# An adaLN transformer block on one core: first transfers reordered, modulation products moved, next tile's input prepared one slot ahead

## The reference

```python
x = L0_attn_x                                             # (8, 1024, 512)
mod = (_silu(L0_c) @ L0_wmod).reshape(8, 6, 1, -1)        # one row per batch: 6 x 512
sa, ca, ga, sb, cb, gb = (mod[:, i] for i in range(6))
ga, gb = sign(g) * maximum(abs(g), 0.25)                  # for both gates
h = _layernorm(x) * (1 + ca) + sa
x = x + ga * attention(h)                                 # 16 heads of 32
h = _layernorm(x) * (1 + cb) + sb
x = x + gb * feed(h)                                      # dense + shared LoRA + 2 of 6 routed LoRAs
```

## Time and profile before

| | us |
|---|---|
| median of 3 runs | 2372.66 (2369.42 to 2372.81) |
| the profiled execution | 2375.0 |
| its span, first to last instruction | 2373.1 |
| PE busy | 2145.7 (90%) |
| DVE busy | 1749.7 (74%) |
| ACT busy | 1340.7 (56%) |
| POOL busy | 788.2 (33%) |

### The profile page before, as it was taken

One profiled execution on the slowest core, in us unless ns is written; L12 is line 12 of the kernel. 1 busy time (PEld: TensorE's weight loads), 2 busy tenths in 40 slices (PEclk: granted clock), 3 DMA queues, 4 the chain that ended last, 5 costly groups with the idle time before them and its releaser, 6 DMA issues.

```text
span 2373.1 us, 48974 instructions
## 1 busy us (share of the span) xinstructions
PE 2145.7 (90%) x17944; PEld 1427.3 (60%) x17944; DVE 1749.7 (74%) x4740; ACT 1340.7 (56%) x4701; POOL 788.2 (33%) x780
## 2 busy tenths in 40 slices
PE   4888999899998999989999899989999899997887
PEld 0665666566665666656665566656666566664454
DVE  3456888768886788768887688866887678875776
ACT  1244666556665566646656566655666556663664
POOL 0333333343333233333332433324333423333221
PEclk9998999999999999989999899999999999997989
DMA  6010000200011000110001100020001100011000
GB/s 233 19 40 15 23 28 24 68 22 28 28 32 63 28 24 28 46 49 19 28 28 41 54 28 24 23 76 24 22 25 45 50 28 28 24 46 45 19 19 19
DMA packets 48892, 89.64 MB, mean 38 GB/s; under 512 B 6760, under 2 KB 6760, under 8 KB 48656
## 3 DMA queue, kind: packets, MB, share of 16 engines
q1 hardware_dynamic: 39440, 69.74, 9.6%
q10 hardware_dynamic: 9216, 16.78, 1.9%
HBM read 69.68 MB, written 16.83 MB: 36 GB/s over the span
## 4 chain that ended last, share of the span: by engine, by line
PE 63%; DVE 22%; ACT 6%; issue 5%; POOL 2%; DMA 1%; SPq 0%; DVEq 0%; ACTq 0%; POOLq 0%
PE ps_m L702 9%; PE ps_o L634 7%; PE ps_m L506 6%; PE ps_m L667 5%; PE ps_m L507 5%; PE ps_m L508 5%; PE ps_s L628 4%; PE ps_t L610 4%; DVE ps_s L1548 4%; ACT pw L1033 3%; PE ps_m L684 3%; DVE wmax L1553 3%; PE ps_s L597 3%; PE ps_s L586 3%; PE ps_m L705 2%
## 5 line engine op out<-in xcount | busy, mean ns | idle before, releaser
L1033 ACT ACTIVATE pw<-ps_s,wmax 128x128 f32<-128x128 f32 x1024 | 360.3, 382 | 168.5 <-DVE wmax L1553 168.4
L506 PE MATMUL ps_m<-w_hi,h_hi 128*128 128x512 f32 x768 | 374.0, 487 | 35.1 <-DVE rbf L1520 18.9
L1043 ACT ACTIVATE pw<-pw,wden 128x128 f32<-128x128 f32 x1024 | 313.2, 401 | 5.0 <-DVE wden L1563 4.8
L507 PE MATMUL ps_m<-w_lo,h_hi 128*128 128x512 f32 x768 | 309.7, 403 | 0.0
L508 PE MATMUL ps_m<-w_hi,h_lo 128*128 128x512 f32 x768 | 308.5, 402 | 0.0
L1067 ACT ACTIVATE pT<-ps_s 80x512 f32<-80x512 f32 (+7 forms) x240 | 141.9, 591 | 255.6 <-PE ps_o L634 155.7
L1311 POOL TENSOR_TENSOR h_lo<-hT,h_hi 128x512 fp32r<-128x512 f32 x57 | 72.3, 1268 | 540.4 <-ACT h_hi L993 540.4
L702 PE MATMUL ps_m<-wbt_s,h2T 128*128 128x512 f32 x512 | 249.0, 604 | 0.0
L667 PE MATMUL ps_m<-wo_s,aT 128*128 128x512 f32 x512 | 247.8, 609 | 0.0
L1574 DVE COPY_PREDICATED pT<-keep_prev,ps_t 128x512 f32<-128x512 uint32 x224 | 164.3, 733 | 94.2 <-PE ps_t L610 90.2
L1033 ACT ACTIVATION_READ_ACCUMULATOR pw<-ps_s,wmax 128x1 f32 x1024 | 226.6, 221 | 0.0
(11 more groups left out here) (187 smaller groups left out, 4341.9 us busy)
## 6 DMA issues: line engine op xcount, KB each, us to landing
xa<-x_in SPq DMA_DIRECT2D x65, 256.0 KB, 3.0
xc<-x_in SPq DMA_DIRECT2D x64, 256.0 KB, 2.8
out<-t ACTq DMA_DIRECT2D x64, 256.0 KB, 2.0
wo_s<-wo_in SPq DMA_DIRECT2D x8, 1024.0 KB, 6.3
wbt_s<-wbt_in SPq DMA_DIRECT2D x8, 1024.0 KB
gbc<-gate_rows SPq DMA_DIRECT2D x24, 256.0 KB, 5.4
pw<-wmod_in SPq DMA_DIRECT2D x3, 1024.0 KB, 5.5
pT<-wmod_in SPq DMA_DIRECT2D x3, 1024.0 KB, 5.3
```

The lines of the kernel that those rows point to most:

```text
L506: pe_.matmul(ps[:], h_hi[:, c, :], w_hi[:, col, c, :], start=(c == 0), stop=False)
L507: pe_.matmul(ps[:], h_hi[:, c, :], w_lo[:, col, c, :], start=False, stop=False)
L1033: ins = act.activation(pw[:, hw, :], ps_w[:, j, i, 1, :], ACT.Exp, bias=wmax[:, hw:hw + 1], accum_out=wden[:, 0, hw:hw + 1])
L1043: act.activation(pw[:, hw, :], pw[:, hw, :], ACT.Copy, scale=wden[:, 2, hw:hw + 1]).then_inc(wn_ok, 1)
```

## The change

1. **First transfers.** SP issues only c, the constants, two modulation blocks, one tile of x and the three projection weights (each with a semaphore of its own) at first. The 15 small tables and the masks are issued from ACT's queue, ahead of its first activation. The gate rows, masks and other setup buffers move to other tiles of SBUF.
2. **Modulation.** Only the products 0 and 1 (shift and scale of the first norm) are made before the first tile. The products 2, 5, 3, 4 are made inside `head(0)` to `head(5)` (`mod_part`), with a fifth bank, and their transposes in `head(6)`. The tables and gate rows on DVE move into the heads too. The first K waits only for its own split weights.
3. **One slot ahead.** HT, `h_scaled` and `split_h` of the next tile are done at the end of a slot, no more at the start of its own. The turn does it for tile 0 of the batch after.
4. **Orders.** Banks and the order of units on every engine are rewritten, in the epilogue too. In `first_slot` the four transposes of the compressed probabilities of tile 0 all go to `ps_t`, where before they alternated between `ps_t` and a bank of `ps_s`.

What it computes is the same, instruction for instruction, but for the place of the work. The core of the diff:

```diff
-FIRST_ORDER = [("HT", 0), ("Q", 1), ("K", 0), ("QT", 1), ("Y", 1), ("G", 0),
-               ("KT", 1), ("H2T", 0), ("Z", 0), ("F", 0), ("ZT", 1), ("V", 1)]
+FIRST_ORDER = [("Q", 0), ("K", 1), ("QT", 0), ("G", 1), ("Y", 0), ("KT", 0),
+               ("H2T", 0), ("Z", 1), ("F", 0), ("ZT", 1), ("V", 1), ("HT", 0)]
-TURN_ORDER = [("Y", 0), ("HT", 1), ("Q", 1), ("K", 0), ("V", 1), ("QT", 0),
-              ("KT", 0), ("H2T", 0), ("Z", 1), ("G", 0), ("F", 1), ("ZT", 0)]
+TURN_ORDER = [("Y", 1), ("Q", 0), ("K", 0), ("V", 1), ("QT", 0), ("KT", 0),
+              ("H2T", 0), ("G", 1), ("Z", 0), ("F", 0), ("ZT", 1), ("HT", 1)]
...
+SETUP_UNITS = [("MOD0", 0, 0), ("MOD1", 0, 1), ("MODT", 0, 0)]
+HEAD_EXTRA = {0: [("MOD2", 0, 4)], 2: [("MOD5", 0, 4)], 4: [("MOD3", 0, 4)], 5: [("MOD4", 0, 4)], 6: [("MODT2", 0, 4)]}
...
 def t_spare(t, g):
-    return t > 0 or g % 2 == 0
+    return t > 0
...
             def mod_part(t):                                  # PE, first thing in head(t)
+                if t < 4:
+                    mod_rows(2 if t < 2 else 5, [0, 1] if t % 2 == 0 else [2, 3])
+                elif t < 6:
+                    mod_rows(t - 1)
+                else:
+                    mod_columns("MODT2", 3)
...
             def slot(seg, b, s):                              # PE
                 cs_scores(b, s)
-                transpose_h(seg, b, t, Ta)
                 output(seg, b, t, [0])
                 window_scores(b, s, 0)
-                output(seg, b, t, [1, 2, 3])
-                project(seg, b, t, "Q", 0, [0, 1, 2, 3])
+                output(seg, b, t, [1])
+                project(seg, b, t, "Q", 0, [0])
+                output(seg, b, t, [2, 3])
+                project(seg, b, t, "Q", 0, [1, 2, 3])
                 window_scores(b, s, 1)
...
+                transpose_z(seg, b, t)
+                feed(seg, b, t, [3, NC])
+                transpose_cs(b, s, 3)
+                project(seg, b, t, "V", 2, [0, 1])
+                transpose_h(seg, b, t + 1, Ta + 1)
                 cs_values(b, s, 2)
                 window_values(b, s, 3)
                 cs_values(b, s, 3)
-                project(seg, b, t, "V", 2, [3])
+                project(seg, b, t, "V", 2, [2, 3])
...
             def slot(seg, b, s):                              # ACT
-                h_scaled(seg, b, t, "HT", hT, mod_a, moda_ok, ba + 1)
-                split_h(seg, b, t, Ta)
                 window_exp(b, s, 0)
...
                 probs_copy(b, s, 0)
+                window_norm(b, s, 1)
+                copy_z(seg, b, t)
                 gate_exp(Ta)
-                copy_z(seg, b, t)
                 router_exp(b, t)
...
-                window_norm(b, s, 1)
                 probs_copy(b, s, 3)
+                h_scaled(seg, b, t + 1, "HT", hT, mod_a, moda_ok, ba + 1)
                 copy_out(b, s)
+                copy_v(seg, b, t)
+                split_h(seg, b, t + 1, Ta + 1, t)
                 store(seg, b, t)
-                copy_v(seg, b, t)
```

607 lines of the change are left out of this document (328 added, 279 removed).

## The result

The changed kernel takes 2414.9 us (median of 4 runs, 2413.8 to 2416.9), the kernel before 2372.7 us on the same chip: ratio 1.0178, 95% interval 1.0161 to 1.0196. Forecast were 2326 and a range of 2288 to 2360. The change makes the kernel 1.8% slower; I had given that 0.1.

What follows compares the result with a forecast made beforehand. PE was taken to bound slots and turns, with idle time only in setup and first slots. Terms -32.8 + 1 - 45.5 + 17.5 + 12.6 = -47.2 from 2375.0 gave 2327.8, as a median 2326 us; range 2288 to 2360.

Steps and rivals of the forecast that it cites:

- the prologue's turn: First turn, after the prologue: +1 us for one HT (0.5) and a wait for it.
- Setup and heads, -32.8: Prologue up to the first turn: first Q near 29 us, a gain of 35.7, less 2.9 for products added to heads.
- First slots, -45.5: Seven first slots at -6.5 us each: PE's gap between the halves' scores filled, H2T moved later; bounds -10 and -2.
- The cold spell that I left in the sum: First slots: PE runs at half rate after idling between the halves' scores, costing 2.7 us; assumed to stay.
- my bound of -10: First slots: best case, -10 us each, if the cold spell goes too.
- Slots, +12.6: 42 slots at +0.3 us each, mainly the router late by `window_norm` ahead of `copy_z`; bounds -0.6 and +2.9.
- the slower rival: Slots: norm before `copy_z` on ACT delays router, ZT, F and next HT, up to 2.9 us each; chance 0.1.
- a bound for the first slot only: First slot's -2 bound: DVE's copy of mod_c took 1.24 us against 0.16 while POOL scaled wo_s.
- DVE and ACT have 5 us and more to spare in a slot: Slots: the argument given against the rival that ACT's order makes each slot up to 2.9 us longer.
- Turns, +17.5: Seven turns at +2.5 us each, from waits of V, K and the first half's scores; bounds 0 and +4.
- The waits that I named: Turn: V about 1.4 us late for DVE's read of Y, K 0.6 for Q's bank, scores 0.5 behind cs_scores.
- Epilogue, 0: Epilogue: no change, +-8 us, since its chain from cs_scores to the residual is kept.

Runs made afterwards that it cites:

- e11: Kernel before the change with only the changed kernel's prologue (setup and heads); loop, turn and epilogue as before: 2342.1 us, ratio 0.9874.
- e1: Changed kernel with POOL's `residual_in` moved back behind Q's rotation in first slots (behind `scale_feed` in the epilogue): 2387.8 us.
- e2: Changed kernel with SP loading `xc` for the next batch's tile 0 ahead of wo, POOL's order untouched: 2369.7 us.
- e4: Changed kernel with `copy_z` ahead of half 1's `window_norm` on ACT in slots 2 to 7: 2414.4 us.
- e7: Changed kernel with slots 2 to 7 in the order and bank table of before, HT still prepared a slot ahead: 2391.7 us.
- e5: Changed kernel with half 1's `window_weights` ahead of K's rotation on DVE in slots 2 to 7: 2390.2 us.
- e10: e7 with `final` one place earlier on DVE, ahead of `split_probs` 3: 2383.5 us.
- e13: e10 with `copy_out` ahead of the next HT's scaled copies on ACT: 2406.3 us.
- e6: Changed kernel with the turn's front as before: Y complete on bank 0 ahead of Q, residual ahead of the first rotation: 2416.7 us.
- e15: e6 with DVE's order behind K's rotation in the turn also as before, `ln_a` behind router 1: 2415.7 us.
- e3: Changed kernel with the gate's product in `window_weights` on DVE as a tensor_tensor instead of a tensor_scalar: 2413.0 us.

## Why the prediction was wrong, step by step

The forecast misses by 86 us of span: slots 51.5, first slots 28.3, prologue 4.6, epilogue 3.4, turns 0.6, and -2.5 in the prologue's turn. The numbers below use the table's last column, which has the prediction's own cuts.

- **Setup and heads, -32.8: right in kind, 4.6 too good.** First Q at 31.65 against 29 (range 28 to 34). PE starts at 13.21 and not 11.0, and the third block's transfer holds it 4.16 us ahead of the half product, which I had taken as landed. SP can issue that block only when the first product has freed its buffer (18.61). `h_lo` was ready at 30.46, so about 1.2 us of this reached Q. The heads cost 4.9 and not 2.9. Two steps of my sum do not add up (20.5 + 1.85 is 22.4 and not 22.9, and 22.9 + 2.25 is 25.2 and not 24.9); they nearly cancel. e11 confirms the size.
- **First slots, -45.5: failed, -17.2.** The step that failed is one I did not write down: with `residual_in` ahead of `cs_normalise` on POOL, everything behind it waits for `xc`, which stands on SP behind `wbt` and `wb` and lands 15 us after its own issue. I had worked through PE, DVE and ACT in that slot and let POOL's reordering pass. e1 and e2 show it, 27 and 45 us. With the transfer early (e2) the first slots gain 54.7 us, 7.8 each against my 6.5, and batch 0's gains 9.4. The cold spell that I left in the sum (2.7 us) is not there: 37.55 us of PE at a clock of 1.00 in batch 0 of the changed kernel and in four of the six later ones of e2 (0.96 in the others), against 42.6 at 0.87 before. Batch 0 comes near my bound of -10, which had the cold spell gone; in the other batches the wait for `xc` hid it.
- **Slots, +12.6: failed in size, +64.1.** I named ACT's order as the slower rival and put its threshold at 1.1 us per slot over my 0.3; the slots came out 1.2 over my 0.3, past the threshold. But the mechanism was another: e4 takes exactly that step back and leaves the time as it was. The terms that failed are two. First, the rewritten order, 0.74 us a slot (e7), nearly all of which the place of `window_weights` behind rope K can account for (e5: 0.7); in that chain stands a DVE instruction stretched by 1.0 us, which I had seen once, in the earlier trace rows, and used as a bound for the first slot only. Second, HT a slot ahead. I gave it 0.5 at the back and the same off the front; it costs 0.8 on the mean (e7) and with a better place for `final` still 0.7 (e10). Why is only in part shown: its copies (1.5 us), `copy_out`, `copy_v` and `h_hi` (0.6 each) all want ACT within 3.7 us at the slot's end, and e13 shows that another order moves the wait and does not remove it. Before, HT's copies lay at the slot's front, where ACT had idled. "DVE and ACT have 5 us and more to spare in a slot" was true as a sum and no argument: the spare time was not where it was wanted.
- **Turns, +17.5: +18.1, the number right and the reasons in part.** The waits that I named are there (0.59, 1.09, and 0.39 at the scores against my 0.5). But taking the first two away wins 0.9 us and not 1.7 (e6). Of the 2.57 us per turn the shared banks are 0.9 (e6) and DVE's rear 0.6 (e15); the other 1.1 go with the rest of the order of before, and which part of it holds them is not settled. So the number owes something to luck. `compress` and `select_values` are no longer interleaved on PE, and HT waits 0.60 for `ln_a`; I did not try these apart.
- **Epilogue, 0: +3.4.** `residual_in` ahead of `cs_normalise` in `end_first` is the same fault, and e2 gets 4.9 us back there. But `end_first` is only 1.3 longer than before and `last` 2.5, and epilogues of the same code took 228.5 us (e3) to 233.1 (e6). The 3.4 us are within that.

The range was too narrow for a reason the text itself shows: bounds of the slots were -0.6 to +2.9, which over 42 slots is 147 us, and I let the likeliest value speak for them.

## What to carry to other kernels

When an order is rewritten, follow each moved step on every queue, the idle engine's too: ask what it waits for, down to the DMA queue that issues its input and what stands in front of that, and who stands behind it. An edit repeated 42 times needs its bounds multiplied before its best guess: 1 us per slot outweighs a whole prologue. And when work is prepared ahead, count not the engine's spare time but what else wants that engine in the same few us. When two kernels are compared by stage, cut both at the same work, or a step that crosses the cut passes for a loss.
